# The last expert part of a two-layer decoder: thirteen token tiles through dispatched slots, three through dense rows

## The chip, the cores and the metric

One core of one Trainium2 chip runs the whole program. The metric is the device time of one execution in microseconds (us); "the median" is that of several executions of the same kernel.

## The reference

Two pre-norm decoder layers on x of shape (32, 56, 128), each with self-attention, attention over a context of shape (32, 1500, 128), and a mixture of eight experts of which each token uses two. Every part is added to x. All of it stays as it is; the change concerns the last part, the experts of layer 1:

```python
shared = silu(x @ shared_gate.T) * (x @ shared_up.T) @ shared_down.T      # inner width 256
probs = sigmoid(x @ router_w.T + routing_bias)                             # eight experts
scores, indices = top_k(probs, 2); scores = scores / sum(scores)
w = zeros((tokens, 8)); w[token, indices] += scores
combined = sum over e of w[:, e] * ((silu(x @ gate_w[e]) * (x @ up_w[e])) @ down_w[e])
x = x + shared + combined
```

## The kernel before

The 32 sequences of 56 tokens lie in 16 token tiles of 128 rows, two sequences to a tile, each in 64 rows of which 56 are used. `XR` holds x by rows, `XT` the normed and transposed x (128 features x 2048 columns), `ARENA` everything else. Five engines run programs of their own and meet at semaphores; `Waits.wait_ge` leaves out waits already covered. Six stages follow one another: `l0_attn`, `l0_xattn`, `l0_ffn`, `l1_attn`, `l1_xattn`, `l1_ffn`.

`l0_ffn` (L1026) already sends tokens to their experts. The router's logits are ranked on VectorE (`choose`), counted with matmuls (`count`), and turned into a slot number for each token and choice (`IDX`). GpSimd scatters each token row twice to a list of slots in DRAM (`scatter`, L1524), in which each expert has whole groups of 128 slots. SP loads the slots, TensorE transposes them (`turn_slots`, L1175), VectorE copies the weights of the expert that owns the group into a ring of five (`copy_weights`, L1252), and TensorE runs each group of 128 slots as one expert tile: `up` (L1189) and `down` (L1199). Results are written to DRAM and gathered by GpSimd (L1536); VectorE adds them with their weights (L1393). It takes 42 such tiles (inner width 512) in two chunks.

`l1_xattn` (L1828) runs 32 batches (b) of twelve key tiles (kt, 125 keys each). Its order is written out by hand: `order()` yields steps for every b and kt, `side(b)` adds the chores of a batch at given kt, and every engine walks through the same list and takes its share of each step. Names of steps that matter here: `peak` (a matmul L2147 and the maximum over it on VectorE, L2261), `score` (L2170, then the exponential on ACT, L2341), `apply` (L2186), `own` (ACT copy of the result, L2355), `fold`, `turn`, `out`, `norm`, `finish` (the result of two batches becomes a token tile, is added to x, normed, transposed by L151 and copied to `XT` by L156). `at` gives each step its PSUM bank by a ring. Peaks are made up to two batches ahead into two pairs of banks; keys, blends and masks for a batch are made three to four batches ahead. SP walks the same list; a `pace` wait holds its transfers back to the scores. At ("score", B - 2, 0) SP loads the weights of the last stage.

`l1_ffn` (L2432 on) waits for the whole attention stage. The router (L2490) runs over 16 tiles, ACT takes exp(-logit), and VectorE ranks the experts. Then `experts` (L837) goes through four chunks of 448 token columns and nine experts, the shared one first, so K = 36 steps: four up matmuls (L916) of 448 columns, Silu on ACT (L945), the product on VectorE (L1009), two down matmuls (L928), a copy on ACT (L962), multiplication by the token's weight (L980) and addition (L991) on VectorE; after a chunk, transposes (L900) and the addition to `XR` (L998), then the store (L893). Every expert sees every token.

```python
for k in range(K + 1):
    if k < K:
        n, i = divmod(k, ne)
        x = order[i]
        rhs = real(xT[:, 512 * n:512 * n + 512])
```

## Time and profile before

| | |
|---|---|
| Median of 3 runs | 1519.72 us (1514.0 to 1524.32) |
| Profiled execution, its own time | 1509.65 us |
| Span of that execution | 1507.9 us |
| Mean granted TensorE clock | 0.959 |
| Last attention stage, scores of 32 batches | 607 to 1320.6 us |
| Last expert stage, up to the end | 1326.7 to 1507.9 us |

The span runs from the first to the last instruction; the execution's own time includes what lies around it. PE is TensorE's matmul, PEld its weight load, DVE is VectorE, ACT ScalarE, POOL GpSimd, SP the engine that issues most transfers, SPq its queue. A float32 matmul shows as two instructions. Batches end at their `own` copy: batch 25 at 1207.3, 26 at 1229.0, 27 at 1250.7, 28 at 1270.5, 29 at 1289.4, 30 at 1306.5, 31 at 1320.7 us.

### The profile page before, as it was taken

Reading aid. Unit: us, or ns where it says so; the run is one execution under the profiler, and the core shown is the slowest. Engines: PE = TensorE matmul, PEld = TensorE weight load, DVE = VectorE, ACT = ScalarE, POOL = GpSimd, SP = SyncE. Lnnn points to the kernel's source line nnn. Section 1 sums busy time; section 2 is a strip of 40 time slices with the busy share of each in tenths; the row PEclk is TensorE's granted clock in tenths of the full one; section 3 lists DMA queues with packets and bytes.
Section 4 is the critical chain, followed back from the end, with each engine's and each line's share of the span. In section 5 each row is a group of like instructions: output and inputs, shape, how many; then the busy total and the mean of one; then the engine's idle time right before and its main releaser. Section 6 shows DMA issues by size and latency. Waiting matters only on the chain.

```text
span 1507.9 us, 41832 instructions
## 1 busy us (share of the span) xinstructions
PE 1352.3 (90%) x17179; PEld 923.6 (61%) x17179; DVE 1105.7 (73%) x1832; ACT 820.5 (54%) x1804; POOL 784.4 (52%) x736
## 2 busy tenths in 40 slices
PE   6888999999979985769999999999999999789998
PEld 4557888788946662436656665666666566555554
DVE  6885767757768878648888888888888888335554
ACT  3442344356623431537777777777777777723332
POOL 6675322424676666727777777777777772000000
PEclk9878999999989998879999999999999999989999
DMA  4004400026214034464644464454455454204230
GB/s 129 2 2 130 159 2 2 18 79 192 62 30 72 22 51 94 96 122 122 133 120 130 116 135 123 124 125 127 123 129 130 120 130 105 65 11 104 62 62 13
DMA packets 77088, 134.71 MB, mean 89 GB/s; under 512 B 18081, under 2 KB 56867, under 8 KB 73635
## 3 DMA queue, kind: packets, MB, share of 16 engines
q1 hardware_dynamic: 74850, 127.84, 34.4%
q0 software_dynamic: 2048, 4.20, 0.9%
q8 instruction: 137, 2.24, 0.7%
q14 instruction: 53, 0.43, 0.1%
HBM read 100.54 MB, written 34.73 MB: 90 GB/s over the span
## 4 chain that ended last, share of the span: by engine, by line
PE 42%; ACT 10%; DVE 5%; issue 3%; POOL 1%; DMA 1%; SPq 0%; ACTq 0%; POOLq 0%; DVEq 0%
PE ps L2186 11%; PE ps L916 7%; PE ps L2170 7%; ACT ARENA L2341 4%; PE ps L928 4%; PE ps L2133 3%; PE ps L2124 3%; PE ps L2147 2%; DVE ARENA L2261 2%; ACT ARENA L2319 2%; ACT ARENA L2325 2%; ACT ARENA L2332 1%; PE ps L2195 1%; PE ps L2155 1%; DVE ARENA L2271 1%
## 5 line engine op out<-in xcount | busy, mean ns | idle before, releaser
L2261 DVE TENSOR_REDUCE ARENA<-ps 112x2 f32<-112x1000 f32 x384 | 456.7, 1197 | 116.0 <-PE ps L2147 109.2
L2341 ACT ACTIVATE ARENA<-ps 125x448 f32<-125x448 f32 x768 | 378.3, 549 | 136.6 <-PE ps L2170 135.7
L2391 POOL TENSOR_TENSOR ARENA<-ARENA 64x500 f32<-64x500 f32 x192 | 227.8, 1187 | 109.2 <-ACT ARENA L2319 90.3
L2170 PEld LDWEIGHTS ps<-ARENA 64*125 64x125 bf16 x3072 | 122.6, 134 | 134.4 <-ACT ARENA L2341 71.6
L2170 PE MATMUL ps<-ARENA 64*125 64x112 bf16 x3072 | 169.4, 229 | 20.5 <-ACT ARENA L2341 19.3
L2186 PE MATMUL ps<-ARENA 125*17 125x112 f32 x6144 | 185.6, 262 | 0.0
L127 POOL TENSOR_TENSOR rs<-rs,mhalf 128x1 f32<-128x1 f32 x96 | 73.3, 765 | 178.9 <-DVE rs L122 178.6
L2147 PE MATMUL ps<-ARENA 64*112 64x500 bf16 x768 | 152.7, 387 | 10.0 <-DVE ARENA L2261 9.7
L2186 PEld LDWEIGHTS ps<-ARENA 125*17 125x17 f32 x6144 | 136.8, 98 | 32.2 <-issue 21.9
L2402 POOL TENSOR_TENSOR ARENA<-ARENA 128x500 bf16<-128x500 f32 x96 | 129.3, 1348 | 44.7 <-ACT ARENA L2325 44.7
L2397 POOL TENSOR_TENSOR ARENA<-ARENA 128x500 f32<-128x500 f32 x96 | 122.1, 1272 | 18.0 <-DVE ARENA L2254 11.8
L2124 PE MATMUL ps<-ARENA 128*128 128x500 f32 x192 | 107.3, 642 | 14.7 <-DMA ARENA<-in_ctxT 13.8
L916 PE MATMUL ps<-XT,ARENA 128*128 128x448 f32 x288 | 116.9, 550 | 0.0
L2133 PE MATMUL ps<-ARENA 128*125 128x128 f32 x768 | 110.2, 287 | 0.0
L2133 PEld LDWEIGHTS ps<-ARENA 128*125 128x125 f32 x768 | 93.4, 190 | 23.9 <-issue 22.3
L916 PEld LDWEIGHTS ps<-XT,ARENA 128*128 128x128 f32 x288 | 55.7, 195 | 53.6 <-issue 53.6
L2254 DVE TENSOR_TENSOR ARENA<-ARENA 128x500 f32<-128x500 f32 x96 | 83.3, 867 | 4.9 <-ACT ARENA L2319 4.9
L2319 ACT COPY ARENA<-ps 128x500 f32<-128x500 f32 x96 | 55.7, 581 | 48.1 <-PE ps L2124 44.1
L1009 DVE TENSOR_TENSOR ARENA<-ps,ARENA 128x448 f32<-128x448 f32 x72 | 44.9, 623 | 42.0 <-PE ps L916 40.9
L156 ACT COPY XT<-ps 128x128 f32<-128x128 f32 x96 | 25.6, 271 | 81.9 <-PE ps L151 81.7
L2325 ACT CAST ARENA<-ARENA 128x500 bf16<-128x500 f32 x96 | 58.5, 610 | 21.0 <-POOL ARENA L2397 15.2
L789 POOL TENSOR_TENSOR ARENA<-ARENA 128x896 f32<-128x896 f32 x16 | 27.0, 1690 | 81.1 <-DVE ARENA L718 81.1
(273 smaller groups left out, 2394.9 us busy)
## 6 DMA issues: line engine op xcount, KB each, us to landing
ARENA<-key_parts SPq DMA_DIRECT2D x192, 187.5 KB, 3.7
ARENA<-in_ctxT SPq DMA_DIRECT2D x96, 250.0 KB, 3.6
key_parts<-ARENA SPq DMA_DIRECT2D x64, 375.0 KB, 2.6
ARENA<-token_weights SPq DMA_DIRECT2D x16, 512.0 KB, 5.2
slots<-in_c_blank SPq DMA_DIRECT2D x2, 1472.0 KB, 12.5
results<-ARENA SPq DMA_DIRECT2D x42, 64.0 KB, 3.2
ARENA<-in_L_ffn_W SPq DMA_DIRECT2D x1, 2048.0 KB, 8.6
ARENA<-in_L_ffn_W SPq DMA_DIRECT2D x4, 512.0 KB, 10.3
```

The lines of the kernel that those rows point to most:

```text
L916: e.matmul(ps[:, bk, 0:448], wt(x, c), rhs, start=True, stop=True).then_inc(up_mm.sem, 1)
L2124: e.matmul(ps[:, b1, 0:500], wk, C[b % 3][:, 500 * ch:500 * ch + 500], start=True, stop=True) \
L2133: m = e.matmul(ps[0:KT, b1, 128 * k:128 * k + 128], C[b % 3][:, KT * kt:KT * kt + KT], wv, start=True, stop=True)
L2147: m = e.matmul(ps[0:112, b1 + h, 0:500], Q0[r, b % 3, g].rearrange("p j s -> p (j s)"), KS[b % 4][r, g, 500 * ch:500 * ch + 500], start=Tr ...
L2170: m = e.matmul(ps[0:KT, b1[h], 112 * g:112 * g + 112], KS[b % 4][r, g, KT * kt:KT * kt + KT], Q1[r, b % 2, 112 * g:112 * g + 112], start=T ...
L2186: m = e.matmul(ps[32 * c:32 * c + 17, 3, 112 * u:112 * u + 112], V[b % 3][0:KT, kt, x, :], Pb[0:KT, n % NP_, 112 * x:112 * x + 112], start ...
L2261: e.tensor_reduce(mxp[0:112, b % 2, 2 * g:2 * g + 2, ch], ps[0:112, b1:b1 + 2, 0:500], AX, ALU.max) \
L2325: e.copy(Kh[:, 500 * ch:500 * ch + 500], T1[:, (3 * b + ch) % 3, :]).then_inc(k_hi.sem, 1)
L2341: e.activation(Pb[0:KT, n % NP_, 448 * h:448 * h + 448], ps[0:KT, b1[h], 0:448], ACT.Exp, bias=0.0, scale=1.0).then_inc(exped.sem, 1)
L2391: e.tensor_tensor(T2[r:r + 64, :], T0[64 - r:128 - r, n % 2, :], sin[64 - r:128 - r, sl], ALU.mult) \
L2397: e.tensor_tensor(T1[:, n % 3, :], T1[:, n % 3, :], T2, ALU.add).then_inc(k_sum.sem, 1)
L2402: e.tensor_tensor(Kl[:, sl], T1[:, (3 * b + ch) % 3, :], Kh[:, sl], ALU.subtract).then_inc(k_lo.sem, 1)
```

## The change

Tiles 0 to 12 (26 sequences) go through slots: `LAST_SLOTS` = 30 groups of 128. Their router runs in batches 26 and 27 of the attention stage, the choice on VectorE in batch 28 (33 operations in ten parts, one part a kt, with ACT's exp at kt 0 and the counting matmuls at kt 6), and GpSimd's 26 scatters follow from kt 10 on, one a kt in the list, each waiting only for `IDX`, its rows and the blank list. The constants and the blank list (2.2 MB, DRAM to DRAM) are loaded at the start of the attention stage, the weights at batch 29, the slots at batch 31, where five weight copies and the first eight transposes stand too. The last stage has no wait for the end of the attention stage any more: the close of batch 31 is spread over its first tiles (`tail_kinds`). After 30 expert tiles (down product two tiles behind the up product, three banks for up, `y` copied by ACT) come twelve dense passes: four of the shared expert over 448 columns, whose second product gives rows at once, and eight, one an expert, over the 336 columns of tiles 13 to 15, whose rows are added with their weights from PSUM. The choice for these three tiles (`choose_late`, 19 operations in ten parts) and the additions of the gathered rows (`combine`) lie between them. The norm of tile t is split into `norm`, `scale` (kt 8) and `finish` (kt 9) instead of being finished one tile later. `experts`, `one_hot`, `top1` and the table `token_weights` in DRAM go away.

```diff
@@ -21,6 +21,9 @@
 SPLIT = ((0, 8), (8, 16))
 SLOTS = tuple((2 * 112 * (b - a) + 8 * 127) // 128 for a, b in SPLIT)
 PADS = 256
+LAST_SPLIT = 13
+LAST_SLOTS = (2 * 112 * LAST_SPLIT + 8 * 127) // 128
+LAST_PADS = 448
...
                     f[11].append(("turn", b - 1))
                 if b >= 3 and b % 2:
-                    for kt, step in ((1, "out"), (3, "norm"), (7, "finish")):
+                    for kt, step in ((1, "out"), (3, "norm"), (8, "scale"), (9, "finish")):
...
+                if b == B - 12:
+                    f[3].append(("cast", 0))
+                if b == B - 6:
+                    f[3].append(("route", 0))
+                if b == B - 5:
+                    f[11].append(("route", 1))
+                if b == B - 4:
+                    f[0].append(("exp", 0))
+                    for i, part in enumerate(("chances", "first", "others", "second", "picks")):
+                        f[1 + i].append(("choose", part))
+                    f[6].append(("count", 0))
+                    for i, part in enumerate(("counts", "bases", "places", "table", "shares")):
+                        f[7 + i].append(("choose", part))
+                for n in range(2 * LAST_SPLIT):
+                    at_b, kt = divmod(NK * (B - 4) + 10 + n, NK)
+                    if b == at_b:
+                        f[kt].append(("scatter", n, NK * b + kt))
+                if b == B - 3:
+                    f[6].append(("weights", 0))
+                if b == B - 2:
+                    f[6].append(("clear_pads", 0))
+                if b == B - 1:
+                    f[1].append(("slots_in", 0))
+                    for i in range(5):
+                        f[4 + i].append(("copy_weights", i))
+                    f[9].append(("turn_slots", 0))
+                    f[10].append(("turn_slots", 1))
                 return f
...
                     yield from [x for x in steps if x not in short]
-                yield from (("fold", B - 1), ("turn", B - 1), ("out", NT - 1), ("norm", NT - 1), ("finish", NT - 1))
+                    if n == B * NK:
+                        yield ("begin", 0)
...
                     dst, src = ones(KSb, r)
                     e.dma_start(dst, src).then_inc(c2_in.sem, 16)
+                stages[5].parts["load_consts"](e, w)
                 pace = None
                 for step in order():
-                    if step == ("score", B - 2, 0):
-                        w.wait_ge(*q_step(12))
-                        w.wait_ge(*k_mm(3 * B))
-                        w.wait_ge(*v_mm(3 * B))
-                        w.wait_ge(*k_cos(3 * B))
-                        w.wait_ge(*k_sin(6 * B))
-                        stages[5].run("load", e, w)
...
+            REC, NW, N1 = 768, 5, LAST_SLOTS
+            lo, hi = 0, LAST_SPLIT
+            T, TB = LAST_SPLIT, NT - LAST_SPLIT
+            groups = [(k, min(4, N1 - k)) for k in range(0, N1, 4)]
+            parts_of = ((0, 4), (4, 16), (16, N1))
...
+            turn_bank = lambda g: 6 + g if g < 2 else 1 + g % 2
+            tail_kinds = {"pe": {2: ("fold",), 4: ("turn",), 5: ("out",), 10: ("finish",)},
+                          "dve": {2: ("fold",), 6: ("out", "norm"), 8: ("scale",)},
+                          "act": {4: ("turn",), 10: ("finish",)}}
+            tail_of = {"fold": ("fold", B - 1), "turn": ("turn", B - 1), "out": ("out", NT - 1), "norm": ("norm", NT - 1),
+                       "scale": ("scale", NT - 1), "finish": ("finish", NT - 1)}
+            combine_after = {3: (0,), 4: (1, 2), 5: (3, 4), 6: (5,), 7: (6,), 8: (7, 8), 9: (9,), 10: (10,), 11: (11,), 12: (12,)}
...
+            def load_slots(e, w):
+                w.wait_ge(*scattered(2 * T))
+                for d, (k, n) in enumerate(parts_of):
+                    e.dma_start(XSB[:, k:n], XS[128 * k:128 * n].rearrange("(i p) d -> p i d", p=128)).then_inc(xs_in[d].sem, 16)
...
+            def sp(e, w):
+                for i in range(N1):
+                    w.wait_ge(*y_cp(i + 1))
+                    e.dma_start(YS[128 * i:128 * i + 128], Y[:, i % 8]).then_inc(y_out[i % 8].sem, 16)
+                for k, n in ((0, 4), (4, 8), (8, T)):
+                    w.wait_ge(*combined(n - 1))
+                    store(e, w, k, n)
+                w.wait_ge(*weighed_add(8 * TB))
+                store(e, w, T, NT)
...
+            def up(e, w, i):
+                g, k = divmod(i, 4)
+                bk = up_bank(i)
+                w.wait_ge(*x_cp(g + 1))
+                w.wait_ge(*w_cp(i + 1))
+                w.wait_ge(*free[bk])
...
+                    m = e.matmul(ps[:, bk, 128 * c:128 * c + 128], WT[:, i % NW, 128 * c:128 * c + 128],
+                                 XST[:, g % 3, 128 * k:128 * k + 128], start=True, stop=True)
+                m.then_inc(up_mm.sem, 1)
...
+            def down(e, w, i):
+                bk = 6 + i % 2
+                w.wait_ge(*free[bk])
+                w.wait_ge(*hidden(i + 1))
+                for c in range(2):
+                    m = e.matmul(ps[:, bk, 0:128], hA[:, i % 2, c, :],
+                                 WT[:, i % NW, 512 + 128 * c:640 + 128 * c], start=(c == 0), stop=(c == 1))
+                m.then_inc(down_mm.sem, 1)
...
+            def wide_up(e, w, q):
+                cols, n = columns(q)
+                x = 8 if q < 4 else q - 4
+                for c in range(2):
+                    for u in range(2):
+                        bk = (4 * q + 2 * c + u) % 6
+                        w.wait_ge(*free[bk])
+                        e.matmul(ps[:, bk, 0:n], rec[:, x, 256 * u + 128 * c:256 * u + 128 * c + 128], cols,
+                                 start=True, stop=True).then_inc(wide_mm.sem, 1)
+                        free[bk] = wide_hidden(2 * q + c + 1)
...
+            def wide_out(e, w, q):
+                x = 8 if q < 4 else q - 4
+                bk = 6 + q % 2
+                w.wait_ge(*wide_hidden(2 * q + 2))
+                w.wait_ge(*free[bk])
+                for t in range(4 if q < 4 else TB):
+                    for c in range(2):
+                        m = e.matmul(ps[:, bk, 128 * t:128 * t + 128], hd[:, q % 2, c, 128 * t:128 * t + 128],
+                                     rec[:, x, 512 + 128 * c:640 + 128 * c], start=(c == 0), stop=(c == 1))
...
             def pe(e, w):
-                w.wait_ge(*f1_in(len(loads)))
-                w.wait_ge(*free[6])
-                for t in range(NT):
-                    w.wait_ge(*ln_out(5, t))
-                    m = e.matmul(ps[:, 6, 8 * t:8 * t + 8], xT[:, 128 * t:128 * t + 128], wr, start=True, stop=True)
-                m.then_inc(routed.sem, 1)
-                free[6] = logits(1)
-                x_pe(e, w)
+                for i in range(2, N1 + 2):
+                    if i < N1:
+                        up(e, w, i)
+                    tail(e, w, "pe", i)
+                    if i == 13:
+                        route(e, w, 2, 0)
+                    down(e, w, i - 2)
+                    for g in range(2, len(groups)):
+                        if 4 * g - 3 == i:
+                            turn_slots(e, w, g)
+                w.wait_ge(*weights_in(len(loads)))
+                for q in range(NJ + 1):
+                    if q < NJ:
+                        wide_up(e, w, q)
+                    if q:
+                        wide_out(e, w, q - 1)
...
+            def copy_weights(e, w, i):
+                w.wait_ge(*weights_in(len(loads)))
+                w.wait_ge(*sel(32))
+                if i >= NW:
+                    w.wait_ge(*down_mm(i - NW + 1))
...
+                e.tensor_copy(WT[:, i % NW, :], recs[:, bass.ds(v * REC, REC)]).then_inc(w_cp.sem, 1)
...
+            def multiply(e, w, i):
+                w.wait_ge(*gated(i + 1))
+                if i >= 2:
+                    w.wait_ge(*down_mm(i - 1))
+                e.tensor_tensor(hA[:, i % 2].rearrange("p c n -> p (c n)"), ps[:, up_bank(i), 256:512], sg[:, i % 2, :],
+                                ALU.mult).then_inc(hidden.sem, 1)
...
+            def combine(e, w, t):
+                w.wait_ge(*gathered[t % 8](2 * (t // 8) + 2))
+                w.wait_ge(*shared_add(t // 4 + 1))
+                w.wait_ge(*sel(35))
+                for k in range(2):
+                    if k:
+                        w.wait_ge(*combine_mul(2 * t + 1))
+                    o = 256 * (t % 8) + 128 * k
+                    e.scalar_tensor_tensor(XR[:, t, :], XT[0][:, o:o + 128], GW[:, t, k:k + 1], XR[:, t, :],
+                                           ALU.mult, ALU.add).then_inc(combine_mul.sem, 1)
...
             def dve(e, w):
-                w.wait_ge(*f1_in(len(loads)))
-                w.wait_ge(*routed(1))
-                e.tensor_tensor(L, ps[:, 6, 0:128].rearrange("p (t e) -> p t e", t=NT),
-                                rb.unsqueeze(1).broadcast_to([128, NT, 8]), ALU.add).then_inc(logits.sem, 1)
-                w.wait_ge(*logit_exp(1))
-                e.tensor_scalar(L, L, 1.0, None, ALU.add).then_inc(logits.sem, 1)
-                w.wait_ge(*logits(2))
-                e.reciprocal(L, L).then_inc(logits.sem, 1)
-                w.wait_ge(*logits(3))
-                top1(e, w, L, M1, t1, t8, L2, rev, best)
-                x_dve(e, w)
+                for i in range(N1):
+                    tail(e, w, "dve", i)
+                    multiply(e, w, i)
+                    if i >= 2 and i + 3 < N1:
+                        copy_weights(e, w, i + 3)
+                    if i == 14:
...
+            def result(e, w, i):
+                if i >= 8:
+                    w.wait_ge(*landed(i - 8))
+                w.wait_ge(*down_mm(i + 1))
+                e.copy(Y[:, i % 8], ps[:, 6 + i % 2, 0:128]).then_inc(y_cp.sem, 1)
...
             def act(e, w):
-                w.wait_ge(*logits(1))
-                e.activation(L, L, ACT.Exp, bias=0.0, scale=-1.0).then_inc(logit_exp.sem, 1)
-                x_act(e, w)
-
-            return Stage(load=load, pe=pe, dve=dve, act=act, pool=x_pool, sp=x_sp, end=lambda: x_end)
+                for i in range(1, N1 + 2):
+                    if i < N1:
+                        hide(e, w, i)
+                    tail(e, w, "act", i)
+                    if i >= 2:
...
+                    _, n = columns(q)
+                    for c in range(2):
+                        if q:
+                            w.wait_ge(*wide_hidden(2 * q + c - 1))
+                        w.wait_ge(*wide_mm(4 * q + 2 * c + 1))
+                        e.activation(sgd[:, c, 0:n], ps[:, (4 * q + 2 * c) % 6, 0:n], ACT.Silu, bias=0.0, scale=1.0) \
...
+                    if q == 0:
+                        minus_exp(e, w, 1)
...
+            def scatter(e, w, n):
+                t, k = divmod(n, 2)
+                w.wait_ge(*blank_in(2))
+                w.wait_ge(*ln(NX, 5, t))
+                w.wait_ge(*sel(28))
+                e.indirect_dma_start(XS, bass.IndirectOffsetOnAxis(IDX[:, t, k:k + 1], 0), XN[:, t, :], None) \
+                    .then_inc(scattered.sem, 16)
+
+            def gather(e, w, t):
+                for i in range(N1 - 8, N1):
+                    w.wait_ge(*landed(i))
+                w.wait_ge(*ln(TURN, 5, NT - 1))
+                w.wait_ge(*scattered(2 * T))
+                if t >= 8:
+                    w.wait_ge(*combined(t - 8))
+                for k in range(2):
+                    o = 256 * (t % 8) + 128 * k
+                    e.indirect_dma_start(XT[0][:, o:o + 128], None, YS,
+                                         bass.IndirectOffsetOnAxis(IDX[:, t, k:k + 1], 0)).then_inc(gathered[t % 8].sem, 16)
...
+            def pool(e, w):
+                stages[4].parts["step_pool"](e, w, tail_of["norm"])
+                for t in range(T):
+                    gather(e, w, t)
...
-                for j in {0: (), 2: (1,) if engine == "sp" else (), 3: (1, 2) if engine == "sp" else (1,)}.get(k, (k - 1,)):
+                for j in {0: (), 2: (1,) if engine == "sp" else (), 3: (1, 2) if engine == "sp" else (1,), 5: ()}.get(k, (k - 1,)):
```

## Rows read from the trace of the kernel before

**Rows 1.** The page: busy us, share of the span and instructions of each engine.

```profile
PE 1352.3 (90%) x17179; PEld 923.6 (61%) x17179; DVE 1105.7 (73%) x1832; ACT 820.5 (54%) x1804; POOL 784.4 (52%) x736
```

**Rows 2.** Windows: stretch, us, busy us of PE, PEld, DVE, ACT, POOL; clock, DMA, GB/s.

```profile
1229.00:1250.70 21.70, 20.51 (x358) 13.33 (x355) 18.97 (x25) 16.56 (x38) 15.71 (x14) 1.00 0.47 125
1250.70:1270.50 19.80, 17.52 (x352) 12.65 (x351) 15.91 (x20) 14.29 (x33) 4.81 (x5) 1.00 0.43 101
1270.50:1289.40 18.90, 16.33 (x344) 11.61 (x344) 15.88 (x22) 13.56 (x32) 0.61 (x1) 1.00 0.65 189
...
1306.50:1320.70 14.20, 10.22 (x278) 8.01 (x276) 0.96 (x5) 10.33 (x24) 0.60 (x1) 1.00 0.01 2
1320.70:1333.50 12.80, 8.88 (x41) 7.89 (x42) 2.14 (x9) 1.08 (x4) 1.55 (x2) 0.69 0.00 0
1333.50:1503.50 170.00, 167.31 (x448) 84.91 (x449) 89.73 (x164) 59.94 (x110) 0.00 (x0) 0.98 0.23 54
```

**Rows 3.** Groups by line in batch 28, VectorE: busy us, mean ns; idle before, releaser.

```profile
L2261 DVE TENSOR_REDUCE ARENA<-ps 112x2 f32<-112x1000 f32 x13 | 15.6, 1201 | 4.2 <-PE ps L2147 4.2
```

**Rows 4.** Timeline of hand-over and end: start us, us, engine, line, operation, tiles, count.

```profile
1318.85 1.73 PE L2186 MATMUL ps<-ARENA 125*17 125x112 f32 x64
...
1326.74 6.97 PE L2490 MATMUL ps<-ARENA,XT 128*128 128x8 f32 x32 [0.40 <-ACT XT L156]
...
1504.25 0.69 DVE L998 TENSOR_TENSOR XR<-ps,XR 128x512 f32<-128x512 f32 x1 [1.27 <-PE ps L900]
```

**Rows 5.** Timeline of the dense experts, TensorE.

```profile
1384.70 3.17 PE L916 MATMUL ps<-XT,ARENA 128*128 128x448 f32 x8
...
1387.70 1.67 PE L928 MATMUL ps<-ARENA 128*128 128x448 f32 x4
...
1389.21 3.17 PE L916 MATMUL ps<-XT,ARENA 128*128 128x448 f32 x8
```

**Rows 6.** Timeline of small VectorE operations, first and last expert stage.

```profile
275.27 0.16 DVE L1308 TENSOR_TENSOR ARENA<-ARENA 128x8 f32<-128x8 f32 x1
...
277.20 0.29 DVE L1326 TENSOR_TENSOR ARENA<-ARENA 128x128 f32<-128x128 f32 x1
...
1334.85 0.95 DVE L2503 RECIPROCAL ARENA<-ARENA 128x128 f32<-128x128 f32 x1
```

**Rows 7.** Lines L1524 and L1536: ns min/median/max, first and last start; landing; one scatter.

```profile
L1524 POOL DMA_INDIRECT slots<-ARENA,IDX x32: 956/1010/1432, 279.0 to 366.9; - x32
...
DMA to landing us min/median/max: 2.2/2.3/3.8
...
347.68 0.96 POOL L1524 DMA_INDIRECT slots<-ARENA,IDX  x1 [0.30 <-issue]
...
L1536 POOL DMA_INDIRECT XT<-results,IDX x32: 944/1098/2033, 380.1 to 456.4; - x32
...
DMA to landing us min/median/max: 2.4/2.7/4.2
```

**Rows 8.** DMA issues (KB each, median us to landing) and SP's timeline.

```profile
slots<-in_c_blank SPq DMA_DIRECT2D x2, 1472.0 KB, 12.5
...
583.21 0.78 SPq L2092 DMA_DIRECT2D ARENA<-in_c_ones  x2
...
599.88 2.37 SPq L2072 DMA_DIRECT2D key_parts<-ARENA  x2
```

**Rows 9.** Timeline of the first expert stage, weight loads of `up` and `down`.

```profile
373.63 0.97 PEld L1189 LDWEIGHTS ps<-ARENA 128*128 128x128 f32 x8 [0.92 <-ACT ARENA L1472]
...
374.52 0.97 PEld L1199 LDWEIGHTS ps<-ARENA 128*128 128x128 f32 x8
...
375.41 0.75 PEld L1189 LDWEIGHTS ps<-ARENA 128*128 128x128 f32 x6
```

**Rows 10.** Lines L1252 and L1258: ns min/median/max, first and last start us, forms.

```profile
L1252 DVE COPY ARENA<-ARENA x42: 752/766/932, 322.0 to 411.6; 128x1156 f32 x42
...
L1258 DVE TENSOR_TENSOR ARENA<-ps,ARENA x42: 272/292/294, 332.0 to 417.9; 128x128 f32<-128x128 f32 x42
```

674 lines of the change are left out of this document (422 added, 252 removed).

## The prediction

> **What bounds the kernel now.** I read the page's busy shares first, then the windows over the last batches and the tail, then the timeline of the hand-over, then the groups and single rows that give prices. TensorE is busy 90% of the span [rows 1]; VectorE 73% is the next. In the steady part of the key/value attention (batch 27, 21.7 us) TensorE is busy 20.5 us and VectorE 19.0: TensorE sets the pace with VectorE close behind [rows 2]. From batch 28 on the preparation of later batches runs out: GpSimd falls from 16 us a batch to 4.8 and then to nothing, while VectorE still has 15.9 of 19.8 us, nearly all of it maxima of 1.2 us [rows 2, 3]. Batch 31 has VectorE at 1.0 us of 14.2 and TensorE at 10.2. Then come 12.8 us in which TensorE works through single, dependent steps at a granted clock of 0.69, and 170 us of dense experts with TensorE at 167.3, VectorE at 89.7 and ACT at 59.9. So the last 187.3 us (1320.6, the end of the last attention matmul at 1318.85 + 1.73, to 1507.9) are TensorE time, and nothing hides there [rows 2, 4].
>
> What the dense part buys is readable from its beat: 8 instructions on the way up take 1384.70 to 1387.70, 3.00 us, the 4 down take 1.51; 4.51 us an expert and chunk, 36 of them, 162 us [rows 5]. A float32 matmul is two instructions, so one with 448 columns costs 0.375 us each.
>
> **Part 1, routing moved into the attention.** TensorE gets the router for 13 tiles, 26 instructions. The same 16 tiles take 6.97 us for 32 at the low clock [rows 4], 0.218 each; at the full clock of these batches I take half, 0.11, so 2.9 us, in batches 26 and 27 where TensorE has 1 us spare. All counts: +2.9.
>
> VectorE gets 33 small operations in batch 28 between steps 1 and 11 (by the parts: 2, 4, 3, 3, 2, 4, 4, 4, 4, 3). Their nearest rows are 0.16 us for 8 elements a partition and 0.29 for 128, a reciprocal of 128 0.95 [rows 6]; with 104 and 208 elements in most, I take 0.30 with the hand-off to the next, and 0.6 more for the reciprocal: 10.5 us. VectorE then has 15.9 + 10.5 = 26.4 us of work in a batch of 19.8. Its maxima stand in program order, TensorE can only be two pairs of PSUM banks ahead of them, so the surplus shows: +6.6. Bounds: if the idle time of batches 28 and 29 (3.9 + 3.0 us) absorbs all it can, +3.6; if none is absorbed and the counting matmuls (about 1.5 us) wait their turn as well, +12. I take +6.6, nearest to the single batch. The ACT exponential and these counting matmuls lie beside it.
>
> GpSimd gets 26 scatters from step 10 of batch 28. One is busy 0.96 to 1.43 us, the next follows after 0.30 with nothing waited for, 16 stood in one row so in the first expert stage, landing after 2.3 [rows 7]. 26 x 1.35 = 35 us, in batches 28 (end) to 30, where GpSimd has 0.6 us of work. Batch 31 starts about 38 us after them: hidden, with little to spare. Without that cover the slots come late; that is a rival below. SP's slot load (1.9 MB) is issued at step 1 of batch 31 and its first part is wanted at step 9, some 10 us later. Behind it on SP there is nothing until the first expert result. The seven weight loads stand in batch 29 and land long before batch 31.
>
> In batch 31 five weight copies (2.5 to 3.5 us) fall into VectorE's empty time; TensorE gets 8 transposes and ACT two copies in a batch where both wait for each other in turn: +1.2 (0 to 2.5).
>
> At the start of the attention stage SP gets 9 small loads and a 2.2 MB fill of the slots in DRAM. Fills of 1.4 MB landed in 12.5 us; the next key write is at 599.88, some 16 us after the last issue [rows 8]. SP needs 5 us for 11 issues, so I take 0; if the fill delays key parts in a stage start where TensorE already waits, up to +8.
>
> Splitting the norm of tile t into three steps and finishing it at step 9 takes no more instructions: 0 (-0.5 to +0.5).
>
> Attention ends at 1320.6 + 2.9 + 6.6 + 1.2 = 1331.3.
>
> **Part 2, thirty expert tiles.** 30 = (2 x 112 x 13 + 1016) / 128 rounded down. Each has 4 up and 2 down matmuls with 128 columns, 12 instructions. In the first expert stage 8 instructions start 0.89 us apart (373.63, 374.52, 375.41), 0.111 each [rows 9]: 1.34 a tile, 40.1 for 30. Beside them: 22 transposes of slots 2.4, the close of the last attention batch 1.7, the late router 0.7, one wait for the bank that holds the attention's result 0.6, small hand-offs 1.5. Sum 47.0. The low clock of the old hand-over (0.69 [rows 2]) has no place, since TensorE has work throughout. VectorE must stay under 1.34 a tile: the copy of 1156 elements takes 0.77 and mine of 768 about 0.55, 0.2 to fetch its register, a product of 256 elements 0.43 from 0.29 for 128 [rows 10]; 1.2 us. Tight, but three tiles from 27 to 29 have no copy, and weights are ahead by three. It ends at 1378.3.
>
> **Part 3, the dense passes.** Shared expert: 4 x (8 x 0.375 + 16 x 0.111) = 4 x 4.78 = 19.1. Three last tiles through eight experts: 336 of 448 columns up, 2.25, and 12 x 0.111 = 1.33 down: 8 x 3.58 = 28.7. Ends at 1426.1. Two ACT table changes, the late choice (18 VectorE operations over three passes) and 26 combining operations lie under them.
>
> The 26 gathers start when the last result has landed, about 1382. Busy 1.1 us each and 0.30 between, 1.4, they need 36.4 and 2.7 for the last landing [rows 7]: 1421, before the last pass is through. Hidden by some 6 us.
>
> The Trainium skill, "SBUF — State Buffer" (section "SBUF: two separate sides"), states that GpSimd cannot write the descriptors of its transfers while VectorE runs a float32 SBUF-to-SBUF copy. The trace leans that way: scatters span 0.96 to 1.43 us in a stage with such copies [rows 7, 10]. By that rule scatters (no copies in batches 28 to 30) and gathers (all copies done) go at the low end, 1.26 us, and the gathers end near 1418: the sum stays, the margin is 9 us.
>
> **Part 4, the end.** Three weighed additions and two combining ones, 1.7 us. Before, the last addition ended at 1504.94 and the span at 1507.9, 3.0 [rows 4]; a second pair of stores behind the first, 0.8. Span 1426.1 + 1.7 + 3.8 = 1431.6, against 1507.9: -76.3. That profiled execution took 1509.65, so the like one takes 1433.4. It was the quickest shown: the median of the runs is 1519.72, 10 us above. I put the difference on the median: 1443.4, say **1443**.
>
> **The rivals.**
> A, tiles that wait. In the first expert stage the tiles took (417.9 - 322.0) / 42 = 2.28 us for 16 instructions worth 1.78 [rows 9, 10]; if the same 0.45 of waiting returns, 30 x 0.45 = 13.5: 1457. Against it: the down product is now two tiles behind, not one, and there are three banks. For it: VectorE at 1.2 of 1.34.
>
> B, gathers become the end. The longest took 2.03 us [rows 7]; 26 x 2.33 = 61 from 1382, plus 2.7 and the last addition: 1446 instead of 1428, so 1461. It decides above 1.65 us a gather. Against it: the median of 1.10.
>
> C, the attention pays more: +12 for VectorE and +8 at its start, against 6.6 and 0: 1457.
>
> D, slower than before: each indirect transfer starts only once the one before has landed. With period p, scatters cost 26p - 38 beyond their cover, gathers 26p - 43; 52p - 81 exceeds 76.3 from p = 3.0 on. At 1.0 + 2.7 = 3.7 it is 111: 1554. Landing times speak for it as a possible period; the 0.30 us between two scatters of the old kernel speaks against [rows 7].
>
> **How the numbers follow.** Forecast 0.66, A 0.10, B 0.05, C 0.12, D 0.02; 0.05 for a gain larger than mine (the choice absorbed, -3, and the hand-offs and the start of batch 31 nothing, -3: 1437 and a few less if the run-to-run level is lower). Own range of the forecast 1433 to 1453; with A, B and C 1429 to 1464. About 1% is what this kernel's measurement can tell. Faster by over 1% in all but D and a sliver of joined mishaps: 0.96, same 0.02, slower 0.02.
>
> **What would show it.** Right: batch 28 longer by about 7 us with VectorE over 90% busy; scatters 1.26 to 1.4 us apart, ended before batch 31; a granted clock of 1.0 from batch 31 to the end; the tiles 45 to 49 us, the dense passes 48; the last gather landed before the last pass. Wrong: TensorE idle on VectorE's copies in the tiles (A), the combining additions waiting on DMA at the end (B), idle TensorE on key parts before 700 (C).

## The result, and the profile after

The changed kernel takes **1447.11 us** in the median of 4 runs (1441.98 to 1449.21). The kernel before takes 1516.93 when the runs made beside it are counted in; the ratio is **0.954**, 95% interval 0.951 to 0.958. The forecast was 1443 in a range of 1429 to 1464, own range 1433 to 1453. The profiled execution took 1447.52 us (span 1445.7), against 1509.65 (span 1507.9) before.

The page of the changed kernel, engines (it answers to [rows 1]):

```profile
PE 1286.1 (89%) x17390; PEld 924.4 (64%) x17390; DVE 1084.0 (75%) x1860; ACT 800.7 (55%) x1791; POOL 825.1 (57%) x790
```

TensorE is 66 us less busy with 211 more matmul instructions: the dense float32 ones were long.

Windows of the changed kernel, columns as in [rows 2]: batches 26 to 31, the tiles, the dense passes:

```profile
1211.00:1238.20 27.20, 26.51 (x385) 18.52 (x383) 18.28 (x24) 16.75 (x39) 15.10 (x14) 0.87 0.41 104
1238.20:1260.70 22.50, 20.85 (x359) 13.63 (x357) 19.25 (x26) 16.76 (x39) 16.38 (x15) 1.00 0.50 119
1260.70:1285.80 25.10, 20.33 (x367) 14.85 (x367) 22.61 (x52) 14.29 (x33) 6.79 (x8) 0.93 0.38 86
1285.80:1305.70 19.90, 16.48 (x344) 11.62 (x344) 16.88 (x24) 13.64 (x31) 12.99 (x15) 1.00 0.60 188
1305.70:1325.60 19.90, 15.61 (x311) 11.46 (x311) 7.72 (x16) 12.38 (x29) 11.68 (x12) 0.83 0.28 87
1325.60:1348.30 22.70, 19.24 (x302) 14.47 (x300) 3.40 (x10) 12.88 (x27) 0.18 (x1) 0.63 0.30 75
1348.30:1391.90 43.60, 42.85 (x380) 42.53 (x381) 27.92 (x63) 22.56 (x67) 0.93 (x1) 1.00 0.15 42
1391.90:1440.20 48.30, 48.24 (x259) 36.18 (x257) 30.91 (x91) 14.52 (x28) 24.72 (x26) 1.00 0.18 50
```

The last two rows are full of TensorE work at a granted clock of 1.00, the higher level (2.4 GHz). In the two before them the clock is 0.83 and 0.63, where batches 30 and 31 of the kernel before had 1.00.

Timelines of the changed kernel, the scatters and gathers of GpSimd, SP's slot load, TensorE at the start of the tiles, at their last matmuls and at the first dense one, and VectorE's last combination:

```profile
1281.41 1.08 POOL L2805 DMA_INDIRECT last_slots<-XT,IDX  x1 [13.55 <-DVE IDX L2592]
...
1318.38 0.96 POOL L2805 DMA_INDIRECT last_slots<-XT,IDX  x1 [0.31 <-issue]
...
1323.12 2.14 SPq L2369 DMA_DIRECT2D ARENA<-last_slots  x3
...
1345.26 2.05 PE L2433 MATMUL ps<-ARENA 128*128 128x128 f32 x16
...
1391.48 0.68 PE L2443 MATMUL ps<-ARENA 128*128 128x128 f32 x4 [0.23 <-DVE ARENA L2516]
1392.00 2.42 PE L2469 MATMUL ps<-XT,ARENA 128*128 128x448 f32 x6
...
1395.67 1.02 POOL L2817 DMA_INDIRECT XT<-last_results,IDX  x1 [37.13 <-DMA last_results<-ARENA]
...
1427.07 0.94 POOL L2817 DMA_INDIRECT XT<-last_results,IDX  x1 [0.30 <-issue]
...
1441.05 0.73 DVE L2687 SCALAR_TENSOR_TENSOR XR<-XT,GW,XR 128x128 f32<-128x128 f32 x2
```

The tiles last from 1345.26 to 1392.0, 46.7 us (forecast 47.0); the dense passes to 1440.2, 48.2 (47.8); the rest 5.5 (5.5). The last gather starts 14 us before the last combination. So everything behind the attention came as forecast to half a microsecond, and the attention is where the forecast failed: the tiles start 24.7 us later than the old attention ended (1320.6), not 10.7.

The stretch between the copies of the attention's own-key result (`e.copy(Om, ...)`, one a batch, read from the timeline) divides those 24.7 us (the last copy itself comes at 1348.3, some 3 us behind the first tile's first matmul). The same reading for kernels of the experiments, which the next section takes up; E stands for the number in the label, and each column is one profiled execution:

| us | before | after | E5 | E9 | E7 | E6 | E8 | E10 | E12 |
|---|---|---|---|---|---|---|---|---|---|
| batch 2 ends at | 706.2 | 705.0 | 705.1 | 713.5 | 700.0 | 708.1 | 709.1 | 725.8 | 726.5 |
| batches 4 to 25 | 479.4 | 483.9 | 485.6 | 485.8 | 480.5 | 485.7 | 484.5 | 482.0 | 482.5 |
| 26 | 21.6 | 27.1 | 25.7 | 26.5 | 24.4 | 22.4 | 26.5 | 22.4 | 23.3 |
| 27 | 21.8 | 22.5 | 22.6 | 22.5 | 22.6 | 22.6 | 22.7 | 22.6 | 22.5 |
| 28 | 19.8 | 25.1 | 26.2 | 24.5 | 24.5 | 24.8 | 24.7 | 28.2 | 31.7 |
| 29 | 18.9 | 19.9 | 19.4 | 19.5 | 19.5 | 19.9 | 19.9 | 49.4 | 34.1 |
| 30 | 17.1 | 19.9 | 18.4 | 17.1 | 19.9 | 17.9 | 17.1 | 18.2 | 21.4 |
| 31 | 14.2 | 22.8 | 22.8 | 18.4 | 22.8 | 18.2 | 24.1 | 18.2 | 18.2 |
| from there to the end | 187.2 | 97.4 | 97.3 | 97.4 | 97.4 | 97.4 | 97.4 | 110.4 | 99.1 |

To read what follows: the experiments form five groups, each run on one chip and each on another, and the kernel before took 1530.12 us beside E1 to E4, 1516.85 beside E5 and E6, 1519.94 beside E7 to E9, 1534.29 beside E10 and E11, 1529.26 beside E12. So times are compared within a group, and ratios to the kernel before across groups. One of E6's four executions (1509.63 us, clock 0.83) was in a slower state and is left out of its figure.

### The profile page after: what moved, and what is told of

The parts are those of the page before. It is cut to its first block, busy times and chain, and to the rows that moved or that the text cites. A ratio compares the mean times of both kernels' runs of the same rounds, so it can differ in the third digit from the quotient of the medians.

```text
span 1445.7 us, 42359 instructions
## 1 busy us (share of the span) xinstructions
PE 1286.1 (89%) x17390; PEld 924.4 (64%) x17390; DVE 1084.0 (75%) x1860; ACT 800.7 (55%) x1791; POOL 825.1 (57%) x790
## 3 DMA queue, kind: packets, MB, share of 16 engines
q8 instruction: 139, 2.28, 0.7%
## 4 chain that ended last, share of the span: by engine, by line
PE 36%; ACT 9%; DVE 9%; issue 4%; POOL 2%; DMA 1%; SPq 0%; ACTq 0%; DVEq 0%; POOLq 0%
PE ps L2010 9%; PE ps L1994 7%; ACT ARENA L2170 4%; DVE ARENA L2086 4%; PE ps L1957 3%; PE ps L1948 3%; PE ps L1971 3%; PE ps L2469 2%; PE ps L2433 2%; ACT ARENA L2154 2%; ACT ARENA L2148 2%; ACT ARENA L2161 1%; PE ps L2019 1%; POOL ARENA L2221 1%; PE ps L2480 1%
## 5 line engine op out<-in xcount | busy, mean ns | idle before, releaser
L2221 POOL TENSOR_TENSOR ARENA<-ARENA 64x500 f32<-64x500 f32 x192 | 232.3, 1210 | 110.9 <-ACT ARENA L2148 92.6
L1994 PE MATMUL ps<-ARENA 64*125 64x112 bf16 x3072 | 172.5, 232 | 24.6 <-ACT ARENA L2170 17.0
L2010 PE MATMUL ps<-ARENA 125*17 125x112 f32 x6144 | 191.4, 267 | 0.0
L2010 PEld LDWEIGHTS ps<-ARENA 125*17 125x17 f32 x6144 | 140.4, 99 | 35.1 <-issue 26.1
L2232 POOL TENSOR_TENSOR ARENA<-ARENA 128x500 bf16<-128x500 f32 x96 | 114.7, 1195 | 63.9 <-ACT ARENA L2154 63.9
L1957 PEld LDWEIGHTS ps<-ARENA 128*125 128x125 f32 x768 | 93.5, 190 | 24.8 <-issue 22.2
L2161 ACT COPY ARENA<-ps 125x512 f32<-125x512 f32 x96 | 57.1, 594 | 20.9 <-PE ps L1957 20.8
L1971 PEld LDWEIGHTS ps<-ARENA 64*112 64x112 bf16 x768 | 54.9, 131 | 18.6 <-DVE ARENA L2086 16.7
L1267 ACT ACTIVATE ARENA<-ps,ARENA 128x128 f32<-128x128 f32 x168 | 47.9, 371 | 25.2 <-PE ps L977 25.2
```

Source lines behind the costliest of these rows:

```text
L1957: m = e.matmul(ps[0:KT, b1, 128 * k:128 * k + 128], C[b % 3][:, KT * kt:KT * kt + KT], wv, start=True, stop=True)
L1971: m = e.matmul(ps[0:112, b1 + h, 0:500], Q0[r, b % 3, g].rearrange("p j s -> p (j s)"), KS[b % 4][r, g, 500 * ch:500 * ch + 500], start=Tr ...
L1994: m = e.matmul(ps[0:KT, b1[h], 112 * g:112 * g + 112], KS[b % 4][r, g, KT * kt:KT * kt + KT], Q1[r, b % 2, 112 * g:112 * g + 112], start=T ...
L2010: m = e.matmul(ps[32 * c:32 * c + 17, 3, 112 * u:112 * u + 112], V[b % 3][0:KT, kt, x, :], Pb[0:KT, n % NP_, 112 * x:112 * x + 112], start ...
L2221: e.tensor_tensor(T2[r:r + 64, :], T0[64 - r:128 - r, n % 2, :], sin[64 - r:128 - r, sl], ALU.mult) \
L2232: e.tensor_tensor(Kl[:, sl], T1[:, (3 * b + ch) % 3, :], Kh[:, sl], ALU.subtract).then_inc(k_lo.sem, 1)
```

## The experiments

**E1, the norm split alone, on the kernel before.**

```diff
-                    for kt, step in ((1, "out"), (3, "norm"), (7, "finish")):
+                    for kt, step in ((1, "out"), (3, "norm"), (8, "scale"), (9, "finish")):
...
+                elif kind == "scale":
+                    ln_scale(e, w, 5, step[1])
```

> The kernel before with one part of the change alone: the norm of a token tile is split into norm, scale (kt 8) and finish (kt 9). In the changed kernel batches 4 to 25 last 0.18 us longer each than before, 4.0 us in all, and the split is the only part of the change that touches them. If the split is the cause, the ends of batches 4 to 25 drift by 3 to 4.5 us here too and the time is 1519 to 1521. If the cause lies elsewhere (place of the buffers, the rows kept in XT0), the drift stays under 1 us and the time is that of before, 1515 to 1518.

Measured 1534.4 (10 runs) against 1530.12 beside it, ratio 1.0034 (1.0005 to 1.0063): the split costs some 5 us by itself (1 to 10 by the interval); the forecast of 1519 to 1521 had counted from another chip's level. Batches 4 to 25 take 485.0 there against 479.4, somewhat more than the 3 to 4.5 expected. (Batch 31 also takes 17.0 us there against 14.2, at a granted clock of 0.77 against 1.00, though none of the new work stands in it.) In batches 4 to 25 the place is one line. The scaling operation in batches 3 to 25, of the kernel before, of E1 and of the changed kernel, one fence each (ns min/median/max, first and last start us):

```profile
L143 DVE TENSOR_SCALAR xn<-XR,mv,rs x11: 337/346/347, 753.5 to 1189.5; 128x128 f32<-128x128 f32 x11
```

```profile
L143 DVE TENSOR_SCALAR xn<-XR,mv,rs x12: 1280/1286/1287, 731.1 to 1216.2; 128x128 f32<-128x128 f32 x12
```

```profile
L146 DVE TENSOR_SCALAR XT<-XR,mv,rs x12: 1280/1282/1284, 717.2 to 1201.0; 128x128 f32<-128x128 f32 x12
```

The operation is the same, it takes 1.28 us in place of 0.34, and every one of the 12 does. The timelines of VectorE and GpSimd in the changed kernel show what it meets:

```profile
1069.75 1.28 DVE L146 TENSOR_SCALAR XT<-XR,mv,rs 128x128 f32<-128x128 f32 x1
...
1069.65 1.29 POOL L2227 TENSOR_TENSOR ARENA<-ARENA 128x500 f32<-128x500 f32 x1
```

At step 8 it starts 0.1 us behind GpSimd's addition of two halves of a later batch's keys and ends when that ends (1071.03 and 1070.94), and so in all 12; at step 3, where it stood before, it takes 0.34. The Trainium skill, "SBUF — State Buffer" (section "SBUF: two separate sides"), says that GpSimd and a VectorE instruction that runs in a 2-port performance mode or has two SBUF inputs hold a shared pair of ports as an exclusive lock, so that whichever starts first blocks the other for its whole instruction. The trace agrees as far as the waiting goes: 0.94 us lost each time; which mode the scaling ran in no run here shows. 12 times 0.94 are 11 us of VectorE. What reaches TensorE stands at the transposes (L154) of the changed kernel in batches 3 to 25, in a row of what its engine waited for before them:

```profile
  DVE XT L146: 4.8, 11
```

TensorE waited 4.8 us for the scaling in 11 waits, as much as the 4.5 us by which batches 4 to 25 are longer. The split also moves the transpose and the copy from step 7 to step 9, and no run moves these without the scaling.

**E2, the router in small groups**, on the changed kernel: tiles 0 to 2, 3 to 5, 6 to 8 and 9 to 11 in batches 20, 22, 24 and 26 in place of twelve tiles in batch 26.

```diff
-                if b == B - 6:
-                    f[3].append(("route", 0))
+                for k, at_b in enumerate((B - 12, B - 10, B - 8, B - 6)):
+                    if b == at_b:
+                        f[3].append(("route", (3, 4, 5, 0)[k]))
```

> The changed kernel with the router's 24 matmul instructions of 8 columns not in one block in batch 26 but six at a time in batches 20, 22, 24 and 26. Theory 1 (the block of narrow matmuls makes TensorE's granted clock fall to its low level for some 7 us, and that costs half of what batch 26 lost): the clock stays at 1.0 from batch 20 to 27, batches 20 to 27 lose 3.0 to 3.6 us in all against 9.2 us less the drift of 1.4 now, and the kernel gains 2 to 3 us on the changed one. Rival (the work itself costs it, 24 instructions that queue behind ACT's exponentials): the same 5 to 6 us, only spread, and the same time within 1 us.

**E3, matmuls of no use** in batches 30 (from step 6) and 31 (to step 8), 15 of 512 columns into a PSUM bank, on the changed kernel.

```diff
+                elif kind == "warm":
+                    w.wait_ge(*peaked(12 * B))
+                    w.wait_ge(*ks_of(B - 1))
+                    e.matmul(ps[:, 4, 0:512], stages[5].parts["oneb"], KS[3][:, 0, 0:512], start=True, stop=True)
```

> The changed kernel with 15 bfloat16 matmuls of 512 columns into a PSUM bank that nobody reads, one a step from kt 6 of batch 30 to kt 8 of batch 31 (0.21 us each at the full clock, 3.2 us of TensorE). They compute nothing. Theory 1 (batches 30 and 31 are long because TensorE's granted clock is at the low level for 24 us there): the clock stays at 1.0 in batch 31, batches 30 and 31 up to the first expert tile shrink by 5 to 8 us, the kernel gains 4 to 8 us on the changed one although it does more. Rival (the slots' load, five weight copies, ACT's two copies and eight transposes in batch 31 make it long): no gain, or 1 to 3 us lost to the added work, also where the clock is 1.0.

**E4, each scatter waits for the landing of the one before.**

```diff
                 w.wait_ge(*sel(28))
+                if n:
+                    w.wait_ge(*scattered(n))
```

> The changed kernel with each scatter waiting until the one before has landed. Theory (what makes the scatters free is that they leave without a wait): the period goes from 1.26 us to 0.96 + 2.3 + 0.1, about 3.4 us, the last lands near 1370 instead of 1322, TensorE finds no slots at the end of batch 31, stands idle some 25 to 35 us, and the time is 1472 to 1485. Rival (scatters have slack enough behind the attention): under 5 us lost.

Measured: E2 1499.78, E3 1505.3 (ratios 0.978, 0.973 to 0.983, and 0.983, 0.977 to 0.988), E4 1508.69 in a single run; all three missed their forecasts. They are 53 to 62 us above the changed kernel's 1447.11, of which the chip's level (1530 for 1517) is some 13; the rest nothing in the edits of E2 and E3 explains. E4 shows two things, though. Its scatters start at 1299.88 to 1382.12, 3.3 us apart in the mean, and a row of the waits says what that holds up:

```profile
DVE XT L146 <- POOL rs L130: 26.1, 1, 26.1
```

The reciprocal root of the last tile's norm is GpSimd's and stood behind the waiting scatters in its program; VectorE waited 26 us for that 0.6 us operation, TensorE's transpose behind it 22, and batch 31 took 49.1 us against 22.8. Half of rival D is seen here: what the change saves by not waiting is not the scatters' own time but whatever is queued behind them.

E2 and E3 have a batch 29 of 49 and 48 us. E5 and E6 had to say whether that was theirs.

On its own question E2 says: batch 26 takes 22.4 us at a clock of 1.00, but batches 4 to 26 together take 509.0, against 509.8 in E3 and 508.6 in E4, which have the router in one piece. Spreading it gave nothing there that one trace each can tell. E3 has batches 30 and 31 at 36.3 us and a clock of 0.98 and 1.00, E2 without the matmuls of no use at 34.2 and 0.98 and 1.00: the clock stood without them, and they cost 2 us.

**E5, the changed kernel unchanged, and E6, E2's and E3's edits together.**

> The changed kernel itself, beside the experiments, because the three kernels built on it lost some 35 to 45 us in batches 29 to 31 and in the dense passes that the profiled changed kernel did not (all three engines stand still about 12 to 17 us while GpSimd's scatters run on, then TensorE issues single matmuls 0.35 to 0.7 us apart, and no packet of the instruction queue is recorded for 28 us). Theory 1, the loss is one of the instruction fetch and belongs to the chip or the moment and not to an edit: about 1485 to 1510 here, with a stretch of over 15 us without PE work in batches 28 to 31. Theory 2, it belongs to the edits (their code has shifted where blocks of instructions begin): 1447 +- 8, with no such stretch.

> The router in groups of at most 9 small operations in batches 20, 22, 24 and 26 and 15 matmuls of no use in batches 30 and 31, on the changed kernel. If the low granted clock in batches 27 and 30 to 31 is what the attention stage lost, and DVE blocks are what lowers it: without an instruction stall 1447 - 3 (batches 26 and 27) - 7 to 10 (batches 30 and 31) = 1434 to 1437; with the stall of theory 1 it is 10 to 13 us under the unchanged kernel of this same call. If the low clock is only a symptom of the waits between TensorE and ScalarE: no difference to the unchanged kernel beyond 3 us.

Measured: E5 1438.04 (ratio 0.945, 0.939 to 0.951), without a stall; E6 1441.07 (0.950, 0.942 to 0.957), without one either. Theory 1 had expected a stall here too; theory 2 fails by E6, which has both edits and no stall. So the stall is not of the edits. In the trace of E6 batch 26 takes 22.4 us and not 25.7, and batches 30 and 31 36.1 and not 41.2. The windows of these two in E6 (columns as in [rows 2]):

```profile
1305.56:1323.48 17.92, 13.71 (x311) 10.04 (x311) 7.24 (x15) 12.41 (x29) 11.04 (x11) 1.00 0.26 79
1323.48:1341.66 18.18, 14.68 (x306) 11.44 (x309) 3.87 (x11) 12.92 (x27) 0.82 (x1) 1.00 0.43 109
```

The clock stays at 1.00, but the two ratios overlap and E6's is not the lower one. One trace each was too little, as E9 then showed.

**E9, the changed kernel once more, E7 and E8 beside it.** E7 puts scale and finish back to one tile late for tiles 0 to 10 and splits only from batch 25 on, where the routing needs the last tiles; E8 pauses at every sixth scatter and third tile's gathers.

```diff
-                    for kt, step in ((1, "out"), (3, "norm"), (8, "scale"), (9, "finish")):
-                        f[kt].append((step, (b - 3) // 2))
+                    t = (b - 3) // 2
+                    f[1].append(("out", t))
+                    f[3].append(("norm", t))
+                    if 1 <= t <= 11:
+                        f[3].append(("scale", t - 1))
+                        f[7].append(("finish", t - 1))
+                    if t >= 11:
+                        f[8].append(("scale", t))
+                        f[9].append(("finish", t))
```

```diff
+                if n and n % 6 == 0:
+                    w.wait_ge(*scattered(n))
...
+                if t and t % 3 == 0:
+                    w.wait_ge(*gathered[(t - 1) % 8](2 * ((t - 1) // 8) + 2))
```

> The changed kernel itself, as the thing to compare the next two with. If the stall of all engines seen in the first three kernels built on it belongs to one chip: 1435 to 1450 on a chip where the kernel before takes about 1517, and 1485 to 1510 where it takes about 1530.

> The changed kernel with the norm's scaling, transpose and copy put back to where the kernel before has them (one tile late) up to batch 23, and split only from batch 25 on, where the routing needs it. The split alone cost 1.0034 of the kernel before, about 5 us, over 15 tiles. Theory 1 (it costs each tile a little, in the attention beats): 11 of 15 tiles get it back, -3.5 to -4 us against the unchanged kernel of this call, and in the trace batch 25 ends 4 us earlier. Theory 2 (the drift of 4 us up to batch 25 has another source, such as the router's preparations): no difference, within 1 us, at batch 25.

> A wait for the landing of the one before at each sixth scatter and each third tile's gathers: 4 pauses of about 1.7 us in each train. My theory, that these trains have slack (11 us at the end, 13 before the tiles): no difference to the unchanged kernel, within 2 us. If a train starves the instruction fetch (a chip where the kernel before takes 1530): 20 to 40 us under the unchanged kernel there. Rival, the sending without waits is what the change lives on: 5 us or more slower, the pauses adding up to the start of the tiles or to the last combination.

Measured: E9 1449.46 (0.956, 0.952 to 0.960), within its forecast; E7 **1435.0** (0.946, 0.942 to 0.951), E8 1452.71 (0.958, 0.954 to 0.961).

E7 gets back what E1 said: its batches 4 to 25 take 480.5 against 485.8, and the operation is short again:

```profile
L146 DVE TENSOR_SCALAR XT<-XR,mv,rs x12: 334/338/340, 746.4 to 1192.4; 128x128 f32<-128x128 f32 x12
```

That is 5 us, theory 1. The other 9 of the 14 us between the medians are not its doing as far as the traces tell: batch 2 ends at 700.0 in E7's and at 713.5 in E9's, ahead of the first line in which they differ, while in batches 30 and 31 E7's trace has the low clock and is 7.1 us longer than E9's.

E9 also has a window that E5 and the first trace did not have, of the very same kernel (batches 30 and 31):

```profile
1314.45:1331.56 17.11, 12.81 (x313) 9.50 (x311) 7.23 (x15) 12.34 (x29) 11.02 (x11) 1.00 0.29 89
1331.56:1349.95 18.39, 14.89 (x302) 11.53 (x298) 3.87 (x11) 12.86 (x27) 0.82 (x1) 0.91 0.42 109
```

35.5 us at 1.00 and 0.91, against 42.6 at 0.83 and 0.63 in the first trace, with the same work (x313 and x302 against x311 and x302). TensorE's busy time grows by the same 7 us, 34.9 for 27.7. So the low clock costs 7 us there, and it comes and goes without any edit. E6's full clock is therefore no proof for its fillers.

E8's median is 3.3 us above E9's, which the two intervals do not tell from nothing; its trace refutes my slack of 13 us ahead of the tiles. GpSimd's and TensorE's timelines in it:

```profile
1298.19 0.95 POOL L2807 DMA_INDIRECT last_slots<-XT,IDX  x1 [2.01 <-DMA last_slots<-XT,IDX]
...
1312.06 0.96 POOL L2807 DMA_INDIRECT last_slots<-XT,IDX  x1 [6.61 <-DMA last_slots<-XT,IDX]
...
1341.39 1.11 PE L2422 MATMUL ps<-ident,ARENA 128*128 128x128 f32 x4 [2.94 <-DMA ARENA<-last_slots]
```

A pause is 2.0 us, and 6.6 where the seven weight loads fill the queues at that moment. The last scatter starts at 1334.80, SP can issue the slot load only at 1337.10, the transposes of the slots wait 3.9 us for it in two waits, and batch 31 takes 24.1 us against E9's 18.4 (at a clock of 0.79 against 0.91). The gathers' pauses cost nothing (97.4 in the last row of the table).

**E10, all three edits (E7's, E2's, E3's), and E11, the same without the matmuls of no use.**

> The changed kernel with the split of the norm only from batch 25 on, the router in groups of at most 9 small operations, and the 15 matmuls of no use in batches 30 and 31. From the traces so far: batches 3 to 25 480.5 (485 unsplit removed), batch 26 22.4, batches 30 and 31 36.1, in all 606 +- 2 for batches 3 to 31 (the changed kernel 621, 620 and 614), and 97.4 from there to the end as in every trace; 1430 to 1436 if the stages before take what they took in the changed kernel (batch 2 ends at 705 to 713), and faster than both kernels. If the low clock is not kept off by the fillers: 612.

> The kernel before this one in the list without the matmuls of no use. Theory 1 (without them TensorE's granted clock falls to half in batches 30 and 31): the segment of some 20 us at 0.5 is back, batches 30 and 31 take 41 to 43 instead of 36, and the median is 3 to 6 us above the one with them. Theory 2 (the fall comes and goes by itself: one of three traces of the unchanged kernel had only 3 us of it): no difference in the medians, within 1.5 us.

Measured: E10 1493.17 (0.974, 0.971 to 0.977), E11 1497.44 (0.978, 0.975 to 0.982). Neither forecast holds, for the stall is back (batch 29: 49.4 and 49.5). Outside of it, batches 30 and 31 take 34.2 us without the fillers (clock 0.97 and 1.00) and 36.3 with them (0.98 and 1.00): as in E2 and E3, the fillers cost 2 us there, and the clock stood without them. The 4 us between the medians the other way have no place in the traces. What lowers the clock in these batches stays open.

Beside a kernel before of about 1530, the stall now stands in all four traces with unspaced scatters (E2, E3, E10, E11), and E4 has it in its gathers; beside one of 1517 to 1520, it stands in none of six. Each chip had one group of runs only, so chip and moment cannot be told apart; "kind of chip" below is short for these two cases. What happens in it, GpSimd and TensorE in E10:

```profile
1307.95 1.03 POOL L2821 DMA_INDIRECT last_slots<-XT,IDX  x1 [0.20 <-issue]
...
1335.02 0.96 POOL L2821 DMA_INDIRECT last_slots<-XT,IDX  x1 [0.30 <-issue]
...
1324.35 0.67 PE L2004 MATMUL ps<-ARENA 64*125 64x112 bf16 x8 [11.71 <-issue]
...
1331.33 0.36 PE L2020 MATMUL ps<-ARENA 125*17 125x112 f32 x1 [0.18 <-issue]
1332.03 0.38 PE L2020 MATMUL ps<-ARENA 125*17 125x112 f32 x2 [0.34 <-issue]
1332.71 0.34 PE L2020 MATMUL ps<-ARENA 125*17 125x112 f32 x1 [0.31 <-issue]
1333.41 0.53 PE L2020 MATMUL ps<-ARENA 125*17 125x112 f32 x2 [0.36 <-issue]
```

While the scatters run on 1.27 us apart, TensorE stands 11.7 us with nothing to wait for, and then gets matmuls by ones and twos 0.7 us apart where a row of 32 is normal. The queues over 28 us of the scatters (packets, MB, share), in E9 and in E10:

```profile
q1 hardware_dynamic: 4720, 3.54, 42.6%
q0 software_dynamic: 670, 1.37, 14.6%
q8 instruction: 4, 0.07, 1.0%
q14 instruction: 2, 0.02, 0.2%
```

```profile
q1 hardware_dynamic: 4032, 3.20, 36.8%
q0 software_dynamic: 583, 1.20, 12.5%
q14 instruction: 1, 0.01, 0.1%
```

The instruction queues moved six packets in E9 and one in E10. In E10 they have none at all between 1310.5 and 1339.3, and the last scatter starts at 1335.0; in E2 none from 1319.3 to 1347.7 with the last scatter at 1343.5, in E11 none from 1309.2 to 1338.1 with it at 1333.6. The silence ends 4 to 5 us behind the train each time. That made a theory for the last run.

**E12, E10 with a pause at each fourth scatter and second tile's gathers.**

```diff
+                if n and n % 4 == 0:
+                    w.wait_ge(*scattered(n))
...
+                if t and t % 2 == 0:
+                    w.wait_ge(*gathered[(t - 1) % 8](2 * ((t - 1) // 8) + 2))
```

> The kernel of all three edits with, in addition, a wait for the landing of the one before at each fourth scatter and each second tile's gathers. On a chip where the kernel before takes about 1530 (there batch 29 took 48 to 49 us in four kernels with the scatters back to back, and the last passes lost some 13 more): theory 1, a train of indirect transfers without a pause keeps the instruction fetch waiting until it ends: each pause lets one through, batch 29 takes 20 to 25 and the time is 1440 to 1455 instead of 1493. Theory 2, the three engines stand still for another reason than the train (the chip's memory is slower there at that moment): batch 29 stays at 45 or more and the time at 1490 to 1505. On a chip where the kernel before takes about 1517 there is no stall to remove, and the pauses cost what they add to the start of the tiles, some 6 us: 1432 to 1442.

Measured 1475.48 (0.965, 0.962 to 0.967), on a chip of the slower kind (but not E10's chip). That is between the two forecasts. The queues over 28 us of its scatters:

```profile
q1 hardware_dynamic: 4720, 3.54, 42.1%
q0 software_dynamic: 480, 0.98, 10.3%
q8 instruction: 2, 0.03, 0.6%
```

Behind the attention the pauses remove nearly all of it (99.1 us against 110.4, with 97.4 where there is no stall). In batches 28 to 30 they remove a quarter: 87.1 us against 95.8, with 62.6 in E6; the largest idle times of its matmuls are three of 3.4 to 4.1 us, and TensorE waits for ACT in them, which itself stood still for a release that the profile finds on none of the core's engines ("remote"):

```profile
1303.41 0.98 ACT L2184 ACTIVATE ARENA<-ps 125x448 f32<-125x448 f32 x2 [4.75 <-remote]
...
1304.53 0.68 PE L2004 MATMUL ps<-ARENA 64*125 64x112 bf16 x8 [4.11 <-ACT ARENA L2184]
```

So trains of indirect transfers without a pause are at least part of the cause in these groups: pauses shorten the loss. That what they hold up is the fetch of instructions is read from the silent queues and from engines that stand with nothing to wait for; no run shows it by itself, and the 24.5 us that are left in the attention are not explained. The changed kernel itself was never run on such a chip. That it would lose the same there is likely from E3, whose only edit costs some 2 us elsewhere, but not shown.

## Why the prediction was right and where it was wrong

The forecast by its own account was 1433.4 for an execution like the profiled one; that took 1447.5. The 10 us that I then added, since the profiled run of before was the quickest shown, had no counterpart after (its profiled run is no quicker than the median of its runs, 1447.11), and covered most of the miss. The 1443 came 4 us near the median with a sum that was 14 us off, all of it in Part 1: that is luck, and the forecast's range held because of it and of the right Parts 2 to 4.

- **Parts 2, 3 and 4** (tiles, dense passes, end): 100.3 forecast, 100.4 measured. Rival A is out: the register-addressed copy is 561 ns and the product 424, one us of VectorE to a tile of 1.55; TensorE waited for VectorE 0.2 us in all of them. (Its price was mis-subtracted too: 2.28 less 1.78 is 0.50, not 0.45, so 1458.) Rival B is out: gathers 1.25 us apart, at the low end of my prices, done 11 us before they are needed. The clock was 1.00 from the tiles on, as said; in batch 31, for which I had named 1.0 as a sign too, it was 0.63.
- **The norm split, "0 (-0.5 to +0.5)"**: the step that failed. +5 us (E1; back in E7). It takes no more instructions, as I wrote, but each scaling took 1.28 us for 0.34, since it moved beside another engine's instruction, and TensorE waited for it.
- **The router, 2.9 for batches 26 and 27**: 6.3 in the first trace, 4.8 and 5.6 in E5 and E9. My 0.11 a matmul assumed the full clock; 24 of them in one row were 3.21 us, 0.134 each, and the granted clock of batch 26 was 0.87. In E4 and E7, with the same router at a clock of 1.00, batch 26 takes 24.4 and the two batches 3.6 more than before: the size was nearly right, the clock was the rest. In groups of six, the batch takes 22.4 at 1.00 (E6), but batches 4 to 26 together gain 3.2 us on E5 and nothing in E2.
- **VectorE's choice in batch 28, +6.6 (3.6 to 12)**: +5.3 (E9 4.7, E5 6.4), with VectorE at 22.6 of 25.1 us, 90%. The size is right, its sum less so: VectorE's busy time in batches 28 and 29 grew by 7.7 us and not by 10.5, and of batch 28 it stood idle 2.5. With 7.7, my sum gives +3.8.
- **Batches 29 and 30, nothing; the start of batch 31, +1.2**: 1.0, 2.7 and, up to the first tile, 5.6. At or near the full clock the two last batches are 34.2 to 35.5 (E2 and E11, E9) against 31.3, some 3 to 4 for my 1.2; the other 7 of the first trace are the low clock (E9 against it). I had read 1.00 in batches 28 to 31 of the kernel before and given it no price.
- **The stage's start, 0 (to +8)**: batch 2 ends 1.2 us earlier; three traces of the changed kernel spread over 8 us there (705.0, 705.1, 713.5), so no more can be said than that no cost stands out. Rival C had the right sum (the attention pays 24.1, measured 24.7) from the wrong places.
- **Rival D** is refuted by the period, 1.26 us without a wait. E4 and E8 show what the absence of waits is worth in batch 31: 26 us with one at each scatter, some 4 to 6 with four of them. "Hidden, with little to spare" was right for the scatters. The slot load had more than my "some 10 us": its first transpose comes 18 us after its issue, and waits for nothing.

Not among my rivals at all was the instruction fetch. The changed kernel came out at 0.945 (E5), 0.954 and 0.956 (E9) of the kernel before, the kernels built on it and run where the stall is at 0.965 to 0.983.

**A version that beats both in its own group:** E7, 1435.0 us, 0.946 of the kernel before, 14 us under the changed kernel beside it (E9), of which 5 are explained. Across groups it is not ahead: the changed kernel alone reached 0.945 in E5.

## What to carry to other kernels

A step moved within a schedule must be priced where it lands, not by its instruction count: look which instruction of GpSimd runs at that moment if the step is VectorE's, and compare the mean duration of its line before and after. When a bound of two or three us is added to a stage that stands at the full clock, give the clock a price too, and take several traces of the same kernel before believing one segment of it. Before waits are taken out of a train of software transfers, look what is queued behind the waits and what else needs the transfer queues, the instruction stream among it; and time the result on more than one chip, beside the kernel before each time: here a kernel's ratio moved by 0.01 from one to the next without any edit.
